# Transfers that wait part by part, late weights, and a re-ordered program in a one-core transformer tower

## The reference

```python
h = x.reshape(8, 1024, 29) @ W + pe                 # embedding, 128 channels
# causal attention over the 1024 tokens, 8 heads of 16 channels
n = layernorm(h)
Q, K, V = heads(n @ Wq + bq), heads(n @ Wk + bk), heads(n @ Wv + bv)
attn = softmax((Q @ K.T + mask) / 4)
h = h + merge(attn @ V) @ Wo + bo
# feed-forward with a shared expert and 8 routed ones in 2 groups
f = layernorm(layernorm(h)) * ln_scale + ln_bias
shared = swiglu(f @ shared_in.T) @ shared_out.T + shared_b
g = argmax(f @ group_gate.T + group_bias)
top2, weights = top_k(softmax(expert logits of group g + expert_bias), 2)
h = h + shared + sum over the two experts of weight * (swiglu(f @ expert_in.T) @ expert_out[e].T) + biases
```

## Time and profile before

| | us |
|---|---|
| median of 3 runs | 991.77 (988.67 to 992.15) |
| profiled execution | 990.75 |
| its span, first to last instruction | 988.9 |
| mean granted TensorE clock in it | 0.964 |

### The profile page before, as it was taken

One profiled execution on the slowest core, in us unless ns is written; L12 is line 12 of the kernel. 1 busy time (PEld: TensorE's weight loads), 2 busy tenths in 40 slices (PEclk: granted clock), 3 DMA queues, 4 the chain that ended last, 5 costly groups with the idle time before them and its releaser, 6 DMA issues.

```text
span 988.9 us, 17663 instructions
## 1 busy us (share of the span) xinstructions
PE 923.0 (93%) x5646; PEld 548.3 (55%) x5646; DVE 806.7 (82%) x2529; ACT 592.4 (60%) x1365; POOL 376.1 (38%) x526
## 2 busy tenths in 40 slices
PE   5688899899999999999999999999999999999986
PEld 5543346346575656457655646456563665545575
DVE  5899987889789898889779988888978989794453
ACT  4025675364857675666746575665856666676743
POOL 6413324222555335333434234433534353421433
PEclk8689989799999999999999999979999999999999
DMA  4220111200011001110110101110110101100000
GB/s 142 73 65 24 43 33 39 67 8 2 30 50 51 30 13 36 60 52 1 44 44 16 56 3 44 60 49 2 33 49 12 65 13 34 43 1 2 11 12 11
DMA packets 45980, 35.19 MB, mean 36 GB/s; under 512 B 10816, under 2 KB 44608, under 8 KB 45760
## 3 DMA queue, kind: packets, MB, share of 16 engines
q1 hardware_dynamic: 43680, 31.97, 9.9%
q10 hardware_dynamic: 2208, 2.10, 0.7%
HBM read 4.28 MB, written 4.19 MB: 9 GB/s over the span
## 4 chain that ended last, share of the span: by engine, by line
PE 65%; DVE 24%; issue 5%; ACT 3%; POOL 1%; SPq 1%; DMA 1%; DVEq 0%; POOLq 0%; ACTq 0%
PE bank_w L590 10%; PE bank_s L542 10%; PE bank_p L572 9%; DVE bank_s L780 6%; PE bank_f L678 5%; PE bank_f L680 5%; PE bank_f L679 5%; DVE mx_far L776 4%; PE bank_f L476 3%; PE bank_f L478 2%; PE bank_f L477 2%; PE bank_m L644 2%; DVE z L839 2%; PE bank_m L618 2%; PE bank_m L608 1%
## 5 line engine op out<-in xcount | busy, mean ns | idle before, releaser
L1047 ACT ACTIVATE pt<-bank_p 128x512 f32<-128x512 f32 (+3 forms) x768 | 341.3, 493 | 179.1 <-PE bank_p L572 147.7
L780 DVE CUSTOM_DVE_ANT_0 bank_s<-bank_s,causal 128x384 f32<-128x384 f32 (+3 forms) x512 | 242.4, 507 | 42.8 <-PE bank_s L542 41.2
L542 PE MATMUL bank_s<-k_stack,q_stack 96*128 96x512 bf16 (+3 forms) x768 | 223.5, 338 | 24.1 <-DVE mx L780 13.4
L572 PE MATMUL bank_p<-q_stack,k_stack 99*128 99x512 bf16 (+3 forms) x768 | 214.6, 336 | 3.4 <-ACT pt L1047 2.0
L776 DVE TENSOR_REDUCE mx_far<-bank_s 128x1 f32<-128x512 f32 x256 | 164.2, 680 | 15.1 <-PE bank_s L542 14.1
L590 PE MATMUL bank_w<-pt,v 128*32 128x512 f32 (+3 forms) x1536 | 154.3, 511 | 1.7 <-ACT ot L1038 0.6
L1207 POOL TENSOR_SCALAR_AFFINE_SELECT pt<-pt 128x512 f32<-128x512 f32 x128 | 81.7, 640 | 190.2 <-ACT pt L1047 190.0
L542 PEld LDWEIGHTS bank_s<-k_stack,q_stack 96*128 96x128 bf16 x768 | 71.7, 99 | 127.1 <-DVE mx L780 51.4
L572 PEld LDWEIGHTS bank_p<-q_stack,k_stack 99*128 99x128 bf16 x768 | 66.5, 99 | 109.1 <-ACT pt L1047 58.8
L678 PE MATMUL bank_f<-wex_h,hid_h 128*128 128x512 f32 x256 | 117.7, 460 | 0.7 <-DVE gate L932 0.7
L1109 ACT ACTIVATE sel<-sel,wsel 128x128 f32<-128x128 f32 x256 | 81.8, 394 | 42.7 <-DVE sel L951 42.5
(11 more groups left out here) (139 smaller groups left out, 1462.1 us busy)
## 6 DMA issues: line engine op xcount, KB each, us to landing
q_stack<-qk_h SPq DMA_DIRECT2D x96, 64.0 KB, 2.6
k_stack<-qk_h SPq DMA_DIRECT2D x84, 64.0 KB, 2.6
q_stack<-qk_m SPq DMA_DIRECT2D x64, 64.0 KB, 2.6
out<-h SPq DMA_DIRECT2D x16, 256.0 KB, 2.3
k_stack<-qk_m SPq DMA_DIRECT2D x56, 64.0 KB, 2.6
q_stack<-qk_l SPq DMA_DIRECT2D x32, 64.0 KB, 2.6
k_stack<-qk_l SPq DMA_DIRECT2D x28, 64.0 KB, 2.6
x_sb<-x_t SPq DMA_DIRECT2D x16, 64.0 KB, 2.1
```

Source lines behind the costliest of these rows:

```text
L542: nc.tensor.matmul(s_bank[s % 2][:, 0:cols], q_stack[0:STACK, half, hd, t % HT * P:(t % HT + 1) * P], k_stack[0:STACK, hd, key_place(i, ha ...
L572: nc.tensor.matmul(p_bank[p % 2][:, q0:HALF], k_stack[:, hd, key_place(i, kt // HT), kt % HT * P:(kt % HT + 1) * P], q_stack[:, half, hd, ...
L780: nc.vector.tensor_tensor_reduce(src, src, causal[:, HALF - cols:HALF], 1.0, -3.0e38, ALU.add, ALU.max, mx[:, u, col:col + 1]).then_inc(s_ ...
L1047: nc.scalar.activation(pt[:, k % PT_SLOTS, j, q0:HALF], p_bank[p % 2][:, q0:HALF], ACT.Exp, scale=0.25).then_inc(exp_done, 1)
```

## The change

**Waits.** Each of the six transfers of a stack now waits for its own part, and they are issued high parts first. **First weights and constants.** On ACT the rounding of the forward weights and `first_keys` move behind image 0's first fronts. On POOL the other key constant moves out of `constants` to behind the second bias add (item `v` of half 1), and the weights' rests follow that. **Order.** All five strings are changed; no item is added or dropped, and most move by a few places.

```diff
+BY_PART_Q = sorted(range(len(PARTS_Q)), key=lambda n: PARTS_Q[n])
+BY_PART_K = sorted(range(len(PARTS_K)), key=lambda n: PARTS_K[n])
...
     "act": (
-        "iafaaddaaaddppppppppappppappppapppppwpppppppppppawpppppppbppppppppapppppppappppppppppbpppppwpfppppappfpp"
+        "aaaddfaaiaddppppppppppapppappppapppwppppppppppppawpppppppbpppappppppppppppppapppppppbppppppppfppwpappfpf"
...
         def keys(eng, i, half, g):

-            eng.wait_ge(qkl_made, half_no(i, half) * 2 + 2)
             if half and i:
                 eng.wait_ge(st_ready, ((i - 1) * NP_ + UNIT_LAST[2 + g] + 1) * G4)
             elif i > 1:
                 eng.wait_ge(st_ready, ((i - 2) * NP_ + UNIT_LAST[2 + g] + 1) * G4)
-            for n, part in enumerate(PARTS_K):
+            for n in BY_PART_K:
+                part = PARTS_K[n]
+                eng.wait_ge((qkh_made, qkm_made, qkl_made)[part], half_no(i, half) * 2 + 2)
                 eng.dma_start(k_stack[n * DH:(n + 1) * DH, g * G4:(g + 1) * G4, key_place(i, half), :],
...
             def queries(i, half, g):

-                sp.wait_ge(qkl_made, half_no(i, half) * 2 + 1)
                 if i:
                     sp.wait_ge(st_ready, ((i - 1) * NP_ + UNIT_LAST[2 * half + g] + 1) * G4)
-                for n, part in enumerate(PARTS_Q):
+                for n in BY_PART_Q:
+                    part = PARTS_Q[n]
+                    sp.wait_ge((qkh_made, qkm_made, qkl_made)[part], half_no(i, half) * 2 + 1)
                     sp.dma_start(q_stack[n * DH:(n + 1) * DH, half, g * G4:(g + 1) * G4, :],
...
                 pool.wait_ge(const_made, CONSTS)
-                nc.gpsimd.memset(k_stack[STACK:SHIFTED, :, 1:3, :], -1.0).then_inc(other_keys_made, 1)
-                pool.wait_ge(other_keys_made, 1)
...
                     nc.gpsimd.tensor_tensor(mine, mine, bo_sb[:].unsqueeze(1).to_broadcast([P, HT, P]),
                                             ALU.add).then_inc(hb_made, 1)
+                    if n == 1:
+                        pool.wait_ge(hb_made, 2)
+                        nc.gpsimd.memset(k_stack[STACK:SHIFTED, :, 1:3, :], -1.0).then_inc(other_keys_made, 1)
+                        pool.wait_ge(other_keys_made, 1)
```

More of the change, by code:

```diff
@@ L147 @@
[L147 to L151, removed]
@@ new lines @@
+        "hssppwwsppsapspsssfssfspswstpswspsasspsswsppsesppspstspsspwpsbpssspsppsspsppspbspspswwwssbwspsbppsspapps"
+        "wwpsbsspspbspfpfptsspfpwpwppssfsasfspfpsfspfspsfssfssbwsbspfbssppfsspbspfssbsppsfpspptwwsphpwspbspwpsbpp"
+        "sappfppfppfbwwpefpspfsppfssppwppwppsfpspspfpsappsfppsfspafspshsspfspptfswwwpsspfbpsspfbsfbsppsfssbppsfsp"
+        "spawsppwspwwpspasppswpsptpssppeppswwppsbspswspsaspsffspbpfsappffpsswspfspfpfbwssppfpspbfbpsspfbfsspbpspf"
+        "sshppssfppbswwswsspptfsppsffppssbspspfsppsfspfsappswwspwspfspspftwspswppsffpsspapspsfpspsasfpssapsfpssbf"
@@ new lines @@
+        "spshsftspspfssfpssesfspwwwwsppapspspwspsppassppsswsppsspspswpspwsppsbsppspwpspspbpwpspsptspwpspbpspswsbp"
+        "pspspeppspwpspasppwpsspwbspwsspbpspfspfpspffapswwsbfpbfpspbsfpsfbppsfbspspfpsphssppfbfssftspsfssbsppsfsa"
+        "sfsppfspasswwwwsppfsppfsstppfpsapsspfsfppssasppsfpssfpspswwwwssppfspspbfpspsfspshpsspwpssfsppsfpspstffsp"
+        "sfsspesswwwppssbsppspspbpsspwsppwpspbpsspbpwspwpeppssppaspwpsppspwspptwsppsbswssassfspfafsspfppsbpfspafs"
+        "pfspswspsfwpbfbspfbspspfsppsbfbpsfppshsppsfbpswwpssptwpspsfsppsbfsppsapspfpsspwsppswwsppfpfspspfsptspfsp"
@@ new lines @@
+        "assssafsssfshssstssfsseassfasssssssasssassbsssbssstssssbsbssasbassssssbbsbsbfsfbbffsbsfssfsffsbbssbhsfss"
+        "sssbtssbebsfassbssbsfsasfssassfssfasfstfssssassfsssfsssfassfstsssfsssshssfssfsssssfessasssssabssbsssasss"
+        "ssbsbstssbsassssssssasffsbsfssfesfbsfabssbfbssfssbafbssssasssshfsstssfbssbsfbasssssssassftssbssbfssbbsbs"
+        "afssfssafssfssssfsfsssssfssfssstsshsssssfssssfssbssbsssssbbstsssssbsssssssbsbfsbbffbsfsfssfssffsssssfsss"
+        "sfstbbbbbhfbbbffbffffbfffbbfbfbhbffbfbfbfbfffffbffhff"
@@ L197 @@
[L197 removed]
+        "aiaaafappppaapapappapbpapaabppfpfpppccppccapaappppbbafpfpppbccbaccppffaapappccppcpbcpppapbafafabcpcpbcpp"
+        "ffacaapcccpappppcpppppapbabffaapbcppbcpafafcpcccpppcaappcppbppppbaaffaabcpbpcppaffpcacacpcpappcppppapbpp"
+        "cbfafbpabcpacppcafafpcaccpcppappppppbppcbaafafacpcpbpcbpfapafpacpppcpcppppbppbffccppppbcbcpcpfppfcbccbff"
+        "cccccc"
     ),
     "sp": (
[L200 removed]
@@ L201 @@
-        "tddddtctddtddcttccc"
+        "ieedededtdetdtdddttddddtcddtdetddctddtdctdddetddtcdtedctdddeedtddtdctecddtdddtdtddctdddtedcddteteddcddtt"
+        "dcddtddtcdddttctccc"
     ),
```

73 lines of the change are left out of this document (30 added, 43 removed).

## The result

The changed kernel takes 949.58 us (median of 4 runs, 948.52 to 951.46) against 991.09 (4 runs, 988.67 to 992.15): ratio 0.9587, 95% interval 0.9562 to 0.9611. The forecast was 982 with a range down to 968. The direction was right, the size was far off.

A forecast was written before the change was run, and what follows sets the result against it. The start was taken as bound by the chain to the first scores, then DVE; the middle by PE with short waits for DVE and ACT. 990.75 - 6.4 (front) - 2 (order) = 982.35, forecast 982 us, range 968 to 997.

The forecast's parts named there:

- The front: Start of image 0: first score at about 25.6 us, lead 11.4 us, of which 6.4 us is left.
- at the most: Half 1's splits beside POOL's block: both wait, the second for `sel` too, 4.7 us late; 4.5 taken.
- Rival 1: Front's lead stays whole: lead 10.9, order -2, giving 978 us; chance 0.18.
- rival 4: Change hides nothing new: part-wise waits alone worth 1.3 us, time 989; chance 0.21 together with rival 2.
- rival 2: Front's lead is eaten by POOL's block or the passage to image 1: 990 to 992; chance 0.21 with rival 4.
- The order in the middle ... Net -2: Reordered items after the front: 4 us lost on weighing, 6 us gained before scores, net -2 us.
- Scores: PE's idle time before scores in the middle: fewer scores directly following a score, 6 us gained, between 0 and 10.
- Weighing: PE's weighing steps in the middle: 21 more runs cost 4.0 to 6.4 us where PE bounds; 4 taken.
- rival 3: Image passages: broken weighing and new low-clock stretches, up to 8 us each, make it slower, 999 or about 1007; chance 0.16.
- The bound of 10 us: Most the middle's order could gain before scores: 125 of 300 pairs' share of PE's 24.1 us idle.
- In the middle I give the waits nothing: Part-wise waits in the middle: worth 0, since PE's idle time before scores ends mostly with DVE, not a transfer.

The follow-up runs named there:

- e3: Changed kernel with its new order only up to the 60th to 65th score of image 0, the old order from there on: 984.37 us, ratio 0.9942.
- e4: Kernel before plus the part-wise waits, with the new order only from the 60th to 65th score of image 0 on: 955.18 us, ratio 0.9648.
- e2: Changed kernel without the part-wise waits, all six transfers of a stack waiting for the low part again: 963.27 us, ratio 0.9729.
- e1: Kernel before plus the part-wise waits alone, order, constants and weights as before: 990.13 us, ratio 1.0007.
- e9: Kernel before plus the part-wise waits, with 30 POOL instructions made to wait for DVE's normalizations: 982.31 us, ratio 0.9934.
- e17: Kernel before plus the part-wise waits, new order only from the 534th to 578th score, with eight more places of SP's queue: 983.30 us, ratio 0.9939.
- e6: Changed kernel with alternated probs and scores in PE's string made pairs again from the 64th score on: 959.38 us, ratio 0.9695.
- e5: Kernel before plus the part-wise waits, with pairs of probs and scores alternated in PE's string from the 64th score on: 994.37 us, ratio 1.0025.
- e13: Kernel before plus the part-wise waits, POOL waiting for DVE's normalizations and PE's pairs alternated: 986.54 us, ratio 0.9962.
- e14: Kernel before plus the part-wise waits, new order only from the 534th to 578th score, SP's eight places left old: 994.94 us, ratio 1.0048.

## Why the prediction was wrong

- **The front** held in its mechanism. The first score, half 0's splits (0.43 and 0.69 us) and the place of POOL's block came as worked out. Half 1's splits met the block as the prediction's "at the most" has it, `qk_m` beside `wex_l` and `qk_l` beside `sel`. They took 2.22 + 1.63 us, 2.7 more than undisturbed, where 4.5 was taken. But DVE came to them 1.5 us later than worked out (39.25 against 37.8), after it had stood idle 2.0 us for an embedding matmul, a wait that the sum doesn't have. That the front's end came within 1 us (5.6 us ahead, 6.4 forecast) is in part luck, as these two misses offset each other. e3 alone gives 5.9 us. Rival 1, the whole lead, falls; so do rival 4 and rival 2, as the lead lasts to the end.
- **The step that failed is "The order in the middle ... Net -2".** With the waits the order is worth 35 us (e4), without them about 21 (e2 and e3). Its two terms fared differently. Scores: -6 with 10 as the upper bound; PE's idle time in front of them fell by 11.8 us in e4, past the bound, and by 6.7 in the changed kernel, so the term was nearly the right size. Weighing: +4 with bounds of 4.0 to 6.4; with 137 runs no such cost shows, the weight loads' idle time fell from 54.1 us in 178 places to 47.4 in 165. What was absent is a term for the clock: 17.8 of e4's 34.8 us are busy time of PE, and up to 15.6 of these the clock that is no longer withheld. The passage from image 5 to 6 shows how one wait costs more than its length: 1.18 us idle, then some 10 us at half the clock. The prediction had that price in hand (8 us a stretch of 25 us), but only as a danger, in rival 3; the change took such stretches away.
- **The bound of 10 us was built on one kind of item.** The idle time in front of scores is 24.1 of 65.9 us. What PE waits for also stands in front of the forward matmuls (5.4 us for DVE's `gate` before, 2.0 after) and in the clock that follows.
- **"In the middle I give the waits nothing"** was right for the order that the sentence was read from (e1: 0) and wrong for the order it was applied to (e2: 13.7 us). This is the second step that failed.
- **Rival 3** named the right place, the passages between images, with the wrong sign. What spoke against it in the prediction, that scores alternate with other work there, was the better argument.
- How the 35 us divide between collisions, pairs and the rest isn't settled. e9 puts the normalizations' collisions at 8 us in the old order, mostly the passage that e17 wins too, and e6 puts the alternation at 9 to 10 in the new one, but the pieces don't add (e5, e13), so no sum of them is given. Holding the clock up without removing a wait wasn't tried, so that the clock costs the busy time is read from the rows and not shown by a run of its own.

## What to carry to other kernels

When a whole schedule is replaced, price the places where an engine stalls, with everything that it waits for there and the clock in that stretch, not one kind of item over the whole run. A term that is zero in the old order (a transfer that nobody waits for, a collision with slack) has to be priced again for the new one. In a kernel of in-order queues a piece of an order can't be judged alone: moved without the queues that feed it, it can cost (5 us in e14).

## What was not expected of the hardware

- A removed wait can come back as busy time instead of idle time: in e9 DVE lost 11 us of collisions, PE's idle time rose by 2.2 us, its busy time fell by 10.4. At one passage 1.18 us of idle PE was followed by some 10 us at the lower clock level, and without that wait the stretch stayed at 1.00.
- POOL's mask slows a normalization that begins just after it from 0.34 to 0.64 us, and POOL's piled-up work (mask, split, mask) stretched four from 1.1 to 3.0; making POOL wait for DVE there was worth 8 us of 990.
- One transfer that waits at the head of SP's queue (17.6 us) held back another whose data were ready 17 us before it was issued, and PE with it for 10.1 us.
